# Early rows' slots scattered ahead of a subtraction, and the first block multiplied amid the last tile's routing

## What is computed

```python
x = x + gnn(layernorm(x), edges, W, b)          # 20000 edges plus one self edge for each node
flat = layernorm(x)
logits = flat @ router_w.T + router_b
topk_vals, topk_idx = top_k(logits, 2); topk_w = softmax(topk_vals)
for e in range(8):
    cw = sum(where(topk_idx == e, topk_w, 0), axis=-1)
    y = gelu(flat @ w1[e].T + b1[e]) @ w2[e].T + b2[e]
    out = out + y * cw[:, None]
x = x + layernorm(out + flat) * ln_w + ln_b
```

## Time and profile before

| what | us |
|---|---|
| median of 3 runs | 618.37 |
| lowest and highest | 617.83, 619.79 |
| the profiled execution | 617.8 |
| its span, first to last instruction | 615.7 |

### The profile page before, as it was taken

The page is one execution under the profiler, slowest core; times in us unless marked ns, Lnnn a source line. Parts: engine busy times, 40 slices in busy tenths (PEclk is TensorE's granted clock), DMA queues, the critical chain, the costliest instruction groups (busy, mean ns, idle before and its releaser), DMA issues.

```text
span 615.7 us, 12330 instructions
## 1 busy us (share of the span) xinstructions
PE 533.8 (87%) x3660; PEld 298.8 (49%) x3661; DVE 464.7 (75%) x1295; ACT 243.0 (39%) x358; POOL 194.4 (32%) x199
## 2 busy tenths in 40 slices
PE   1799999899999999995879999999999999999100
PEld 1344554445544555553764655556565656564000
DVE  8889869996185888888748678695868685755397
ACT  5334444323271434342634343444443444401480
POOL 3023000000001375746434535343453444151240
PEclk9999999999999999997789999999999999999755
DMA  6873531243237334346367959698888889273878
GB/s 237 322 289 100 155 89 25 56 78 65 50 140 271 137 139 172 138 171 204 90 262 203 296 164 256 217 238 274 208 251 207 258 230 281 29 168 77 264 209 278
DMA packets 59581, 112.34 MB, mean 182 GB/s; under 512 B 33506, under 2 KB 33919, under 8 KB 59520
## 3 DMA queue, kind: packets, MB, share of 16 engines
q1 hardware_dynamic: 49440, 80.02, 37.4%
q0 software_dynamic: 8896, 27.38, 21.3%
q10 hardware_dynamic: 1184, 4.20, 1.9%
HBM read 71.75 MB, written 33.67 MB: 171 GB/s over the span
## 4 chain that ended last, share of the span: by engine, by line
PE 77%; DVE 14%; issue 4%; DMA 3%; ACT 1%; DVEq 0%; ACTq 0%; SPq 0%; POOLq 0%
PE ps L1818 7%; PE ps L1819 7%; PE ps L1943 7%; PE ps L1944 6%; PE ps L1945 6%; PE ps L1922 6%; PE ps L1923 5%; PE ps L1924 5%; PE ps L1728 5%; PE ps L1729 4%; PE ps L1730 4%; PE ps L1655 4%; PE ps L1904 4%; DMA acc_rows<-work,ids_out 1%; DVE wbufs L1574 1%
## 5 line engine op out<-in xcount | busy, mean ns | idle before, releaser
L615 POOL DMA_INDIRECT acc_rows<-work,ids_out x24 | 53.0, 2206 | 107.6 <-DVE work L1510 107.6
L1922 PE MATMUL ps<-rows_and_counts,wbufs 128*128 128x336 f16 (+2 forms) x256 | 76.1, 301 | 3.0 <-issue 2.2
L1924 PE MATMUL ps<-rows_and_counts,wbufs 128*128 128x336 f16 (+2 forms) x256 | 76.1, 301 | 0.0
L1923 PE MATMUL ps<-rows_and_counts,wbufs 128*128 128x336 f16 (+2 forms) x256 | 76.1, 301 | 0.0
L1819 PE MATMUL ps<-wbufs,rows_and_counts 128*128 128x512 f16 x200 | 75.8, 379 | 0.0
L1818 PE MATMUL ps<-wbufs,rows_and_counts 128*128 128x512 f16 x200 | 75.8, 379 | 0.0
L1943 PE MATMUL ps<-wbufs,rows_and_counts 128*128 (+1 forms) x192 | 72.9, 380 | 1.8 <-issue 1.3
L1465 DVE SCALAR_TENSOR_TENSOR wbufs<-stage,wbufs 128x1024 f16<-128x1024 f32 x56 | 67.1, 1218 | 8.1 <-ACT wbufs L933 7.6
L1944 PE MATMUL ps<-wbufs,rows_and_counts 128*128 (+1 forms) x192 | 72.8, 379 | 0.0
L1945 PE MATMUL ps<-wbufs,rows_and_counts 128*128 (+1 forms) x192 | 72.8, 379 | 0.0
L528 POOL TENSOR_TENSOR work<-work 128x1024 f16<-128x1024 f32 x9 | 19.2, 2132 | 164.3 <-ACT work L906 164.3
(11 more groups left out here) (310 smaller groups left out, 1050.5 us busy)
## 6 DMA issues: line engine op xcount, KB each, us to landing
stage<-wst_in SPq DMA_DIRECT2D x72, 512.0 KB
acc_rows<-work SPq DMA_DIRECT2D x10, 512.0 KB
x_rows<-work SPq DMA_DIRECT2D x10, 512.0 KB
wbufs<-b_in ACTq DMA_DIRECT2D x8, 512.0 KB
wbufs<-acc_rows SPq DMA_DIRECT2D x8, 512.0 KB, 5.9
t<-x_in SPq DMA_DIRECT2D x1, 3584.0 KB, 13.2
t<-x_in SPq DMA_DIRECT2D x1, 3072.0 KB, 11.3
t<-x_in SPq DMA_DIRECT2D x1, 2048.0 KB, 7.8
```

Of the source, the lines that this page charges most:

```text
L1922: mm(o, wbufs[:, ds(w + ws, P)], x_hi, start=(j == 0), stop=False)
L1923: mm(o, wbufs[:, ds(w + ws, P)], x_lo, start=False, stop=False)
L1924: ins = mm(o, wbufs[:, ds(w + (LO + ws), P)], x_hi, start=False, stop=(j == DK - 1))
```

## The change

Five edits, all of order; no instruction on data is added or taken away.

1. POOL: at r = FIRST_TILES + 1 = 8, tile 8's subtraction (`xs_lo(18)`) goes behind the two scatters of tile 6, the last of the seven early tiles.
2. Pieces: SP's load, ACT's split and POOL's split stand one tile sooner (r from 0 to 7 instead of 1 to 8).
3. SP: in the same step 8 the load of the early ids (L717) goes ahead of the store of tile 8's xs (L714).
4. PE: block 0 is turned at r = NT, ahead of rank 8, into the bank of `up_ps[3]` (`first_ps`), block 1 at r = NT + 1; then block 0 is multiplied and block 2 turned, and only then comes rank 9. The other blocks follow behind the loop.
5. DVE: block 0's subtraction goes ahead of choose 9, block 1's ahead of place 9; blocks 2 and 3 take the places that blocks 1 and 2 had, and block 3's place behind the second tables falls away.

```diff
@@ POOL
-                if r < NT - 1:
+                if r < NT - 1 and r != FIRST_TILES + 1:
                     xs_lo(NT + r)
...
-                if 1 <= r <= PIECES:
-                    split_lo(PIECES + r - 1, e_hi[0], e_lo[0])
+                if r == FIRST_TILES + 1:
+                    xs_lo(NT + r)
+                if r < PIECES:
+                    split_lo(PIECES + r, e_hi[0], e_lo[0])
@@ SP
-                sp.wait_ge(xs_done, NT + r + 1)
-                sp.dma_start(x2_rows[rows, :], xs.bitcast(F32)).then_inc(x2_first_stored if r < FIRST_TILES else x2_stored, 16)
                 if r == FIRST_TILES + 1:
                     sp.wait_ge(scattered_first, 16 * 2 * FIRST_TILES)
                     sp.dma_start(ids_first[:], slot_table_v[:, 0, 0:len(FIRST)]).then_inc(ids_in, 16)
-                if 1 <= r <= PIECES:
-                    piece(PIECES + STAGES + r - 1, True)
+                sp.wait_ge(xs_done, NT + r + 1)
+                sp.dma_start(x2_rows[rows, :], xs.bitcast(F32)).then_inc(x2_first_stored if r < FIRST_TILES else x2_stored, 16)
+                if r < PIECES:
+                    piece(PIECES + STAGES + r, True)
@@ ACT
-                if 1 <= r <= PIECES:
-                    split_hi(PIECES + r - 1, e_hi[0])
+                if r < PIECES:
+                    split_hi(PIECES + r, e_hi[0])
@@ DVE
             for r in range(NT + 2):
+                if r == NT + 1:
+                    first_turned(0)
                 if 2 <= r:
                     choose(r - 2)
                 if r == NT + 1:
-                    first_turned(0)
+                    first_turned(1)
@@ PE
+            def up_first(j):
+                pe.wait_ge(first_lo_done, j + 1)
...
+                if j + 2 < DK:
+                    turn_first(j + 2, FIRST).then_inc(first_done, 1)
@@ PE, the loop
+                if r == NT:
+                    pe.wait_ge(var_done, len(NORM_GROUPS) + NT)
+                    turn_first(0, FIRST).then_inc(first_done, 1)
                 if r == NT + 1:
-                    for j in range(2):
-                        turn_first(j, FIRST).then_inc(first_done, 1)
+                    turn_first(1, FIRST).then_inc(first_done, 1)
+                    pe.wait_ge(w_lo_done, 2 * PIECES)
+                    up_first(0)
                 if r >= 2:
                     rank(r - 2)
```

More of the change, by code:

```diff
@@ L321, in build, with first_ps @@
         down_ps = [bank(6), bank(7)]
+        def first_ps(j):
+            return up_ps[FK - 1][:, 0:FIRST_CH] if j == 0 else x4_ps[j % 2][:, 0:FIRST_CH]
         act_step5 = sem("act_step5")
@@ L906, in _ @@
                     a.activation(xs[:, 0:D], xn, ACT.Copy).then_inc(xs_hi_done, 1)
-                if 1 <= r <= PIECES:
-                    split_hi(PIECES + r - 1, e_hi[0])
+                if r < PIECES:
+                    split_hi(PIECES + r, e_hi[0])
             def first_turned(j):
                 act.wait_ge(first_done, j + 1)
-                a.activation(x4[:, j * 2 * CH:j * 2 * CH + FIRST_CH], x4_ps[j % 2][:, 0:FIRST_CH], ACT.Copy
+                a.activation(x4[:, j * 2 * CH:j * 2 * CH + FIRST_CH], first_ps(j), ACT.Copy
                              ).then_inc(first_hi_done, 1)
@@ L1405, in _ @@
             v.tensor_tensor(cw[:], cw[:], cw2[:], ALU.add).then_inc(cw_done, 1)
-            first_turned(1)
+            first_turned(2)
             st3.did(v.memset(scan[:], 0.0))
@@ L1426, in _ @@
             st3.wait()
-            first_turned(2)
+            first_turned(3)
             over_e = [1, MAXC, NE]
@@ L1870, in turn_first @@
                     for h in range(2):
-                        ins = mm(x4_ps[j % 2][:, i * P:(i + 1) * P],
-                                 gx0[i].bitcast(F16)[:, h * D + j * P:h * D + (j + 1) * P],
+                        o = first_ps(j)[:, i * P:(i + 1) * P] if tiles == FIRST else x4_ps[j % 2][:, i * P:(i + 1) * P]
+                        ins = mm(o, gx0[i].bitcast(F16)[:, h * D + j * P:h * D + (j + 1) * P],
                                  ident16[:], start=(h == 0), stop=(h == 1), skip_group_check=True)
                 return ins
+            def up_first(j):
+                pe.wait_ge(first_lo_done, j + 1)
+                for f in range(FK):
+                    ws = slice(j * FF + f * P, j * FF + (f + 1) * P)
+                    x_hi, x_lo = [x4[:, at:at + FIRST_CH] for at in (2 * j * CH, (2 * j + 1) * CH)]
+                    o = up_ps[f][:, 0:FIRST_CH]
+                    mm(o, e_hi[0][:, ws], x_hi, start=(j == 0), stop=False, skip_group_check=True)
+                    mm(o, e_hi[0][:, ws], x_lo, start=False, stop=False, skip_group_check=True)
+                    mm(o, e_lo[0][:, ws], x_hi, start=False, stop=(j == DK - 1), skip_group_check=True)
+                if j + 2 < DK:
+                    turn_first(j + 2, FIRST).then_inc(first_done, 1)
             pe.wait_ge(count_hi_read, NG * COUNTS_BY_PE)
@@ L1969, in weights_ready @@
                 settle(pe)
-            pe.wait_ge(w_lo_done, 2 * PIECES)
-            for j in range(DK):
-                pe.wait_ge(first_lo_done, j + 1)
-                for f in range(FK):
-                    ws = slice(j * FF + f * P, j * FF + (f + 1) * P)
-                    x_hi, x_lo = [x4[:, at:at + FIRST_CH] for at in (2 * j * CH, (2 * j + 1) * CH)]
-                    o = up_ps[f][:, 0:FIRST_CH]
-                    mm(o, e_hi[0][:, ws], x_hi, start=(j == 0), stop=False, skip_group_check=True)
-                    mm(o, e_hi[0][:, ws], x_lo, start=False, stop=False, skip_group_check=True)
-                    mm(o, e_lo[0][:, ws], x_hi, start=False, stop=(j == DK - 1), skip_group_check=True)
-                if j + 2 < DK:
-                    turn_first(j + 2, FIRST).then_inc(first_done, 1)
+            for j in range(1, DK):
+                up_first(j)
             pe.wait_ge(slots_done, NT)
```

3 lines of the change are left out of this document (1 added, 2 removed).

## The result

The changed kernel takes 620.6 us in the median of 22 runs (616.89 to 622.5), the kernel before 617.67 us in 22 runs of the same comparison (615.98 to 620.11). The ratio is 1.0040, with a 95% interval of 1.0027 to 1.0053: 2.9 us in the medians, about 2.5 by the ratio, slower. The forecast was 619.7, the range 617.0 to 621.7. So the sign of the forecast and the range held. The size did not: the forecast loss was 1.3 us, the measured one is 2.9, more than twice as much, and by the prediction's own bound of 0.3% this is "slower", to which it gave 0.30 and not 0.58. What matters more is a second fact in these numbers: the kernel before keeps close to 617.7, while the changed kernel has a third of its runs at 616.9 to 618.8 and most of the others at 620 to 622.5.

The account below looks back on a forecast made before the run. PE bounds the kernel, with DVE's routing setting the pace up to 303 us. Terms 0 + 0 + 0.3 (gather) + 1.0 (rank 9 behind block 0) = 1.3 us of loss gave 619.7 us, range 617.0 to 621.7.

Parts of the forecast that it names:

- The early scatter: POOL's scatters of tile 6 at 275.9 and 277.2, 2.0 us sooner; early gathers issued at 281.7 and 283.0.
- The pieces: Weight pieces a tile sooner cost nothing; the weight load gone from ahead of the gathers saves the gather 2.2 us.
- The later subtraction of tile 8: On POOL until 280.4: PE's transposes to 280.4, ACT's copy 0 to 0.1 us, SP's store later; taken as nothing.
- The gather: Second early gather takes 6.8 us, not 8.5, landing at 289.8 (288.6 to 291.5); rank 8 0.3 us later.
- Rank 9 behind block 0: PE ranks tile 9 after block 0's matmuls, at 295.7; DVE's placing at 296.1, 1.0 us later from order alone.
- the sum: Terms 0 + 0 + 0.3 + 1.0 = 1.3 us of loss added to the kernel's time.
- What follows: Behind tile 9's placing DVE gives nothing back; fifth subtraction, PE's last block and third tile's turns stand 1.3 us later.
- Rival 1: Late gather holds rank 8: each microsecond past 289.5 costs one; at the old 8.5 us, 621.4. Chance 0.26.
- Rival 2: PE's clock is at full before block 0, so its 3.09 us halve: 618.2. Chance 0.10.
- Rival 3: Clock falls in PE's gaps behind block 1 or stays low through the third tile: up to 1.5 us more, 621.2. Chance 0.05.
- Rival 4: Unexplained wait between PE's third-tile turns and ACT's answer swallows the 1.3 us: 617.9, or 616.4 without clock fall. Chance 0.13.
- Rival 5: Scatters wait for something other than POOL's subtraction, so the gather isn't earlier and rank 8 waits: 623.3. Chance 0.02.

Follow-up runs that it names:

- the run of the early scatters alone: Kernel before with only tile 6's scatters and the early ids' read moved ahead of tile 8's subtraction and store, weight pieces unmoved: 613.57 us, ratio 0.9979.
- the three profiles of the changed kernel: Profiled executions of the unedited changed kernel, from the first comparison and two repeats: 617.94, 617.48 and 614.76 us.
- the pair with moved instructions: Changed kernel and kernel before, each with 64 tiny unread matmuls in PE's early waits, moving later instructions half a block: 613.96 and 612.14 us.
- the first pair: Changed kernel against the kernel before in the original comparison, 22 runs each: 620.6 against 617.67 us, ratio 1.0040.
- the one upper execution that was profiled: Changed kernel with extra unread matmuls in PE's gaps ahead of blocks 2, 3 and 4; its profiled execution took 620.33 us, median 620.12.
- the run of the order alone: Changed kernel with the queue and weight-piece edits taken back, only the new PE, DVE and ACT order left: 624.33 us, ratio 1.0103.
- with the gaps filled: Changed kernel with 4, 3 and 5 unread matmuls in PE's gaps ahead of blocks 2, 3 and 4: 620.12 us, ratio 1.0064.
- the first four experiments: Changed kernel repeated, 618.95 us; with rank 9 ahead of block 0, 618.44; kernel before with only the queue and piece edits, 616.09; new order alone, 624.33.
- the 64 matmuls: Tiny unread matmuls in PE's first 15 us, shifting later instructions half a block: changed kernel 613.96 us, before 612.14, before with early scatters 611.43.

## Why the prediction was right, and where it was short

**The early scatter:** right. Scatters at 275.97 and 277.26 (said: 275.9 and 277.2), gathers at 281.85 and 283.14 (281.7 and 283.0).

**The pieces:** nothing as a cost, right. The other half of their move, the weight load gone from ahead of the gathers, was sized at 2.2 us, and that was too much: with the load still ahead of it the second gather took 7.3 us in the run of the early scatters alone, and without it 6.6 to 7.2 in the three profiles of the changed kernel, at most 0.7 less. What else took it from 8.5 to 6.6, no run took apart.

**The later subtraction of tile 8:** right, nothing on the path. The transposes moved from 279.80 to 280.45 (said 280.4), with 0.47 us of waiting for POOL.

**The gather:** right in the landing, by terms of which one was too large. It released its turn at 289.74, 289.88 and 290.30 in the three profiles (said 289.8, 288.6 to 291.5), and rank 8 stood at 289.92 in the first (said 290.1); of the 0.3 us for it 0.02 reached DVE (placing of tile 8 at 290.27, before at 290.25). The estimate of 3.2 us from the Trainium skill, "DMA: Bandwidth & Descriptors", section "Anatomy of one DMA", was far off again; the gather took 6.6.

**Rank 9 behind block 0:** the mechanism was right and the term too small. Rank 9 at 295.19 (said 295.7), placing at 295.57 (said 296.1): both half a microsecond earlier than said, since block 0's subtraction stood at 291.70 and not 292.0, and from the first matmul of block 0 to rank 9 it took 2.94 us and not 3.09. The bound for what follows the placing held: nothing was given back (8.58 us from the placing to the fifth subtraction, 8.59 before). In the traces of the pair with moved instructions the term is 1.0 at the fifth subtraction, as in the sum, but in the medians it is 1.8. The profiled execution of the changed one (612.94) is the fastest of its 12 runs, so it shows the smallest case; what adds 0.8 in the others was not caught.

**What follows:** the step that failed. I let everything behind the third tile stand rigid and took the delay of the path for the delay of the kernel. In the first pair 0.78 us of path became 0.2 us of span in the profile and 2.9 us in the medians. Behind it stood a wait that I hadn't read, in both kernels: the fetch of instructions in chunk 1 and chunk 2, 2.2 us of idle time in the profile of before and, by the moved instructions, 3.3 us of its median. The profile's page of the kernel before named it only as idle time released by "issue". With it taken away, the change costs 1.8 us; with it, 2.9 and 2.1 on two other chips. That the remaining 0.3 to 1.1 is this stop taking longer in some runs is likely from the one upper execution that was profiled, but it isn't shown: no profile caught the changed kernel there. So that 620.6 lies in the range is in part luck: the sum gave 1.3 us of loss, and the other 1.6 came from what it didn't have.

**The rivals.** Rival 1 (late gather): the price is right by the run of the order alone, and the landing didn't come to it, but for 0.56 us once. Rival 2 (the clock back before block 0): no, it was at half until 296.85. Rival 3 (the clock falls in the new gaps): no trace of the changed kernel shows it, and with the gaps filled the spread stayed. That the slower runs had the lower clock is so, but where it fell is known of one execution alone, and there it was at 111 us and behind the stop in chunk 1. Rival 4 (the silent wait at the third tile): it happened in the first two profiles and swallowed 0.7 of 0.78 us there, and the second fall of the clock at 313 was missing too (1.00 in the window 310 to 320). It seems to go by the chip: in the first pair and on the chip of the first four experiments (1.5 to 3.7 us from PE's turns to ACT's answer) it is there, on the three others it is not (0.3 us). On two of these three only kernels with the 64 matmuls were profiled, so there the chip and the matmuls can't be told apart; on the third none of four had them. The kernel before took 617.67 and 616.89 us on the first two and 614.86, 615.46 and 615.32 on those. What the wait is stays open. Rival 5: no.

## What to carry to other kernels

A matmul group that another engine waits for goes ahead of work that only fills the array: six tiny matmuls behind twelve large ones cost more than an earlier gather had gained. Where idle time of TensorE has no semaphore and no data transfer behind it, look at the instruction queue in the same microseconds; shifting the program by half a block, with tiny matmuls in an early wait, was worth 3.3 us of 615, more than any edit of order in this study. Before a difference of less than 1% is put down to a change of order, try the shift on both kernels. The fastest kernel of this study is the kernel before with the early scatters and the shifted instructions, 611.43 us, 0.6% below the kernel before; 0.7 us of it are the scatters', with ranges of runs that overlap.

## What the runs showed of the hardware

- TensorE's sequencer stopped for 2.8 to 5.0 us at a block of 16384 bytes of instructions in chunk 1, in eight traces with a DMA share of 0.96 to 1.05; the instructions went on 1.4 to 1.6 us after the packet ended. What was queued in the array hid 2.1 to 2.6 us of each stop.
- In two more traces (rank 9 ahead of block 0, and the early scatters without the pieces' move) the same stop was 2.07 and 2.59 us, and TensorE was not idle at all. What makes the stop longer or shorter from one execution to the next wasn't found.
- With the 64 matmuls ahead, the stop in chunk 1 and TensorE's idle time ahead of both up stages were gone in all four traces.
- Behind an idle time of 2.86 us amid full work TensorE's clock stood at half from 342.93 to 346.35 us (0.83 in the window 340 to 350).
- The second early gather took 8.5 us with a weight load of 512 KB just ahead of it in the kernel before and 7.3 us with the same load in the run of the early scatters alone; with tile 8's store and no load ahead it took 6.6 to 7.2 us in the changed kernel.
